# Differential attention with routed experts: one maximum for both score rows of a unit, and the guard of the denominators twice a batch

## The reference

```python
s1 = einsum('bhqd,bhkd->bhqk', q, k1) * SCALE      # causal: masked above the diagonal
s2 = einsum('bhqd,bhkd->bhqk', q, k2) * SCALE
attn = softmax(s1) - sigmoid(lambda_logit) * softmax(s2)
denom = maximum(sum(abs(attn), axis=-1), 1e-6)
out = einsum('bhqk,bhkd->bhqd', attn / denom, v) @ Wo.T
x = layernorm(x + out)
x = layernorm(x + experts(x) + x)                  # router, top 2 of 8, silu hidden layer of 512
```

## Time and profile before

| what | us |
| --- | --- |
| median of 3 runs | 1231.5 (1228.81 to 1231.53) |
| the profiled execution, its own time | 1223.18 |
| its span | 1221.3 |
| mean granted TensorE clock of the span | 0.952 of 2.4 GHz |

### The profile page before, as it was taken

The page is one execution under the profiler, slowest core; times in us unless marked ns, Lnnn a source line. Parts: engine busy times, 40 slices in busy tenths (PEclk is TensorE's granted clock), DMA queues, the critical chain, the costliest instruction groups (busy, mean ns, idle before and its releaser), DMA issues.

```text
span 1221.3 us, 29361 instructions
## 1 busy us (share of the span) xinstructions
PE 1103.2 (90%) x8786; PEld 725.7 (59%) x8786; DVE 1044.4 (86%) x2722; ACT 915.2 (75%) x2882; POOL 834.0 (68%) x1245
## 2 busy tenths in 40 slices
PE   3788869999899989999899997999899998999897
PEld 1355536666556655666556665666556665566565
DVE  1688788988999899999999899999999999898664
ACT  1688868888688877888688876888678886787232
POOL 2599976776768757877667776777677777677100
PEclk8577779999999999999999999999999999999899
DMA  7503400232005200142003300052002410000000
GB/s 213 126 14 80 99 1 3 62 82 48 1 14 118 70 2 2 36 110 57 1 14 86 89 15 1 21 125 57 1 2 57 89 48 1 19 1 2 1 10 9
DMA packets 62142, 54.66 MB, mean 45 GB/s; under 512 B 6050, under 2 KB 59938, under 8 KB 61986
## 3 DMA queue, kind: packets, MB, share of 16 engines
q1 hardware_dynamic: 61986, 52.78, 17.8%
HBM read 37.03 MB, written 15.73 MB: 43 GB/s over the span
## 4 chain that ended last, share of the span: by engine, by line
PE 66%; DVE 18%; issue 7%; POOL 4%; ACT 2%; SPq 1%; DMA 1%; DVEq 0%; POOLq 0%; ACTq 0%
PE side L809 14%; PE side L803 13%; PE trans L883 12%; PE scores L853 8%; PE heads L872 7%; DVE neg_max L723 6%; PE scores L855 4%; DVE abs_sum L734 3%; PE scores L803 2%; PE scores L809 2%; POOL exps L445 2%; PE side L773 2%; DVE hT L686 1%; DVE xh L566 1%; POOL exps L441 1%
## 5 line engine op out<-in xcount | busy, mean ns | idle before, releaser
L491 ACT ACTIVATE exps<-scores,neg_max 128x256 f32<-128x256 f32 (+3 forms) x1024 | 537.9, 529 | 97.5 <-DVE neg_max L723 80.8
L723 DVE TENSOR_REDUCE neg_max<-scores 128x1 f32<-128x256 f32 (+3 forms) x1024 | 448.7, 479 | 72.8 <-PE scores L855 69.3
L445 POOL TENSOR_TENSOR exps<-exps 128x384 f32<-128x384 f32 (+3 forms) x512 | 444.7, 868 | 42.7
L441 POOL TENSOR_SCALAR exps<-exps,inv_l,lam_l 128x384 f32<-128x384 f32 (+3 forms) x512 | 313.6, 613 | 141.2 <-DVE inv_l L714 138.4
L853 PE MATMUL scores<-stack 72*128 72x256 bf16 (+3 forms) x1024 | 274.1, 314 | 17.5 <-DMA stack<-parts_dram 13.5
L809 PE MATMUL side<-w_sb,hT 128*128 128x128 f32 x1816 | 253.6, 283 | 29.5 <-DVE acc L698 18.1
L883 PE MATMUL trans<-ident,exps 128*128 128x128 f32 x1280 | 254.9, 300 | 22.8 <-ACT diffT L499 19.4
L499 ACT ACTIVATE diffT<-trans 128x384 f32<-128x384 f32 (+3 forms) x512 | 223.4, 436 | 52.9 <-PE trans L883 52.1
L809 PEld LDWEIGHTS side<-w_sb,hT 128*128 128x128 f32 x1816 | 222.6, 192 | 63.7 <-DVE acc L698 29.9
L803 PE MATMUL side<-xnT,w_sb 128*128 128x512 f32 x458 | 247.2, 621 | 1.8 <-ACT xnT L526 1.0
L883 PEld LDWEIGHTS trans<-ident,exps 128*128 128x128 f32 x1280 | 150.4, 147 | 134.7 <-issue 102.5
(11 more groups left out here) (94 smaller groups left out, 685.2 us busy)
## 6 DMA issues: line engine op xcount, KB each, us to landing
stack<-parts_dram SPq DMA_DIRECT2D x288, 96.0 KB
parts_dram<-parts SPq DMA_DIRECT2D x104, 128.0 KB, 2.4
x_in<-x_dram SPq DMA_DIRECT2D x8, 256.0 KB, 4.5
w_sb<-w_dram SPq DMA_DIRECT2D x1, 2048.0 KB, 9.1
x_res<-x_dram SPq DMA_DIRECT2D x8, 256.0 KB, 4.5
o_dram<-y_out SPq DMA_DIRECT2D x8, 256.0 KB, 3.4
wq_sb<-wqT_dram SPq DMA_DIRECT2D x1, 64.0 KB
wq_sb<-wk1T_dram SPq DMA_DIRECT2D x1, 64.0 KB
```

Of the source, the lines that this page charges most:

```text
L441: nc.gpsimd.tensor_scalar(diff[:, q % 2, j, 0:w], exps[:, q % 2, 1, j, 0:w], inv_l2[:, q % 2, j:j + 1], lam_l1[:, q % 2, j:j + 1], ALU.mul ...
L445: nc.gpsimd.tensor_tensor(diff[:, q % 2, j, 0:w], diff[:, q % 2, j, 0:w], exps[:, q % 2, 0, j, 0:w], ALU.subtract).then_inc(diff_done.sem, 1)
L491: nc.scalar.activation(exps[:, q % 2, k, j, 0:w], scores[:, u % 2, k, 0:w], ACT.Exp, bias=neg_max[:, q % 2, j, k:k + 1], accum_out=sums[:, ...
L723: nc.vector.tensor_reduce(neg_max[:, q % 2, j, k:k + 1], scores[:, u % 2, k, 0:w], AX.X, ALU.max, negate=True).then_inc(max_done.sem, 1)
```

## The change

- **Scores.** Where both rows of a unit fit one bank (t = 0 and 1, w = 128 and 256), they are written side by side into the bank of k = 0, by one matmul of 2w columns over both sets of keys, and one of 256 columns for both masks, from a mask that is now held twice. Before it PE waits for both exponentials of unit u - 2. For t = 2 and 3 the four matmuls stay as they were, each k in its bank, and each k waits for its own exponential, save after a packed unit. In every case `score_done` now counts once a unit, after the last of its matmuls.
- **Maxima.** One reduction over both rows, of 2w numbers, with one wait for `score_done` and one `max_done`. Both exponentials of the unit wait for it.
- **Denominators.** `sums` and `abs_sum` are kept for the whole batch; guard and reciprocal run twice a batch, over 32 numbers a row, in slot 40 for the first half and in slot 8 of the next batch for the second, in place of 16 times over 4 numbers.

```diff
-        sums = sb("sums", [P, 4, 2, QUAD])
+        sums = sb("sums", [P, 2, NG, NT, QUAD])
...
+        def packed(t):
+            return 2 * (t + 1) * P <= 512
+
+        def score_pair(u):
+            t = tile_of(u // QUAD)
+            w = (t + 1) * P
+            if packed(t):
+                return scores[:, u % 2, 0, 0:2 * w].rearrange("p (k c) -> p k c", k=2)
+            return scores[:, u % 2, :, 0:w]
...
-                            act.wait_ge(max_done.sem, max_done.after(n, 2 * u + k + 1))
-                            nc.scalar.activation(exps[:, q % 2, k, j, 0:w], scores[:, u % 2, k, 0:w],
+                            act.wait_ge(max_done.sem, max_done.after(n, u + 1))
+                            nc.scalar.activation(exps[:, q % 2, k, j, 0:w], score_pair(u)[:, k, :],
...
-                        q, j = divmod(u, QUAD)
-                        if j == QUAD - 1:
-                            dve.wait_ge(abs_done.sem, abs_done.after(n, 2 * (q + 1)))
-                            nc.vector.scalar_tensor_tensor(out=guard[:, :], in0=sums[:, q % 4, 0, :], scalar=DENOM_MIN,
-                                                           in1=abs_sum[:, q % 2, :], op0=ALU.mult, op1=ALU.max)\
+                        i, last_of_part = divmod(u + 1, DEN_UNITS)
+                        if last_of_part == 0:
+                            part = slice((i - 1) * DEN_G, i * DEN_G)
+                            dve.wait_ge(abs_done.sem, abs_done.after(n, (u + 1) // 2))
+                            nc.vector.scalar_tensor_tensor(out=guard[:, :, :, :], in0=sums[:, 0, part, :, :],
+                                                           scalar=DENOM_MIN, in1=abs_sum[:, part, :, :],
...
-                        for k in range(2):
-                            dve.wait_ge(score_done.sem, score_done.after(n, 2 * u + k + 1))
-                            nc.vector.tensor_reduce(neg_max[:, q % 2, j, k:k + 1], scores[:, u % 2, k, 0:w], AX.X,
-                                                    ALU.max, negate=True).then_inc(max_done.sem, 1)
+                        dve.wait_ge(score_done.sem, score_done.after(n, u + 1))
+                        nc.vector.tensor_reduce(neg_max[:, q % 2, j, :], score_pair(u), AX.X,
+                                                ALU.max, negate=True).then_inc(max_done.sem, 1)
...
+                        if packed(t):
+                            pe.wait_ge(exp_done.sem, exp_done.after(n, 2 * (u - 2) + 2))
+                            nc.tensor.matmul(pair, queries, stack[:, 1:3, QUAD * g + j, 0:w], start=True, stop=False)
+                            nc.tensor.matmul(pair[:, :, w - P:w], ident_bf[:, :], causal_bf[:, :, :],
                                              start=False, stop=True).then_inc(score_done.sem, 1)
+                        else:
+                            before = u - 2 if u >= 2 else u - 2 + UNITS
+                            for k in range(2):
+                                freed = 2 if packed(tile_of(before // QUAD)) else k + 1
+                                pe.wait_ge(exp_done.sem, exp_done.after(n, 2 * (u - 2) + freed))
```

More of the change, by code:

```diff
@@ L58 @@
 LAG_SIDE = 1
+DEN_PARTS = 2
+DEN_G = NG // DEN_PARTS
+DEN_UNITS = UNITS // DEN_PARTS
 SIDE = {}
@@ L179, in build @@
         diffT = sb("diffT", [P, 2, QUAD, T])
-        abs_sum = sb("abs_sum", [P, 2, QUAD])
-        guard = sb("guard", [P, QUAD])
+        abs_sum = sb("abs_sum", [P, NG, NT, QUAD])
+        guard = sb("guard", [P, DEN_G, NT, QUAD])
         inv_den = sb("inv_den", [P, NT, NH])
@@ L392, in body @@
                     for g in range(NG):
[L394 removed]
+                        sp.wait_ge(score_done.sem, score_done.after(n - 1, (g + 1) * QUAD * NT))
                         for z in range(3):
@@ L733, in body @@
                         dve.wait_ge(diff_done.sem, diff_done.after(n, u + 1))
-                        nc.vector.tensor_reduce(abs_sum[:, q % 2, j - 1:j + 1], diff[:, q % 2, j - 1:j + 1, 0:w], AX.X,
+                        nc.vector.tensor_reduce(abs_sum[:, q // NT, tile_of(q), j - 1:j + 1], diff[:, q % 2, j - 1:j + 1, 0:w], AX.X,
                                                 ALU.add, apply_absolute_value=True).then_inc(abs_done.sem, 1)
                     for n, u in units(b, stages, slot, LAG_DEN):
-                        q, j = divmod(u, QUAD)
-                        if j == QUAD - 1:
-                            dve.wait_ge(den_done.sem, den_done.after(n, 2 * q + 1))
-                            nc.vector.reciprocal(inv_den[:, tile_of(q), q // NT:NH:NG], guard[:, :])\
-                                .then_inc(den_done.sem, 1)
+                        i, last_of_part = divmod(u + 1, DEN_UNITS)
+                        if last_of_part == 0:
+                            dve.wait_ge(den_done.sem, den_done.after(n, 2 * i - 1))
+                            nc.vector.reciprocal(
+                                inv_den[:, :, :].rearrange("p t (j g) -> p g t j", g=NG)[:, (i - 1) * DEN_G:i * DEN_G, :, :],
+                                guard[:, :, :, :]).then_inc(den_done.sem, 1)
                     if slot == LAG_PV and "attention" in stages:
@@ L850, in body @@
                             pe.wait_ge(stack_in[g].sem, stack_in[g].after(n, 3 * len(WINDOWS)))
-                        for k in range(2):
-                            pe.wait_ge(exp_done.sem, exp_done.after(n, 2 * (u - 2) + k + 1))
-                            nc.tensor.matmul(scores[:, u % 2, k, 0:w], stack[:, 0, QUAD * g + j, t * P:(t + 1) * P],
-                                             stack[:, 1 + k, QUAD * g + j, 0:w], start=True, stop=False)
-                            nc.tensor.matmul(scores[:, u % 2, k, w - P:w], ident_bf[:, :], causal_bf[:, :],
-                                             start=False, stop=True).then_inc(score_done.sem, 1)
+                        pair = score_pair(u)
+                        queries = stack[:, 0, QUAD * g + j, t * P:(t + 1) * P]
+                        if packed(t):
+                            pe.wait_ge(exp_done.sem, exp_done.after(n, 2 * (u - 2) + 2))
+                            nc.tensor.matmul(pair, queries, stack[:, 1:3, QUAD * g + j, 0:w], start=True, stop=False)
+                            nc.tensor.matmul(pair[:, :, w - P:w], ident_bf[:, :], causal_bf[:, :, :],
+                                             start=False, stop=True).then_inc(score_done.sem, 1)
+                        else:
[3 more added lines that the diff above has]
+                                pe.wait_ge(exp_done.sem, exp_done.after(n, 2 * (u - 2) + freed))
+                                nc.tensor.matmul(pair[:, k, :], queries, stack[:, 1 + k, QUAD * g + j, 0:w],
+                                                 start=True, stop=False)
+                                last = nc.tensor.matmul(pair[:, k, w - P:w], ident_bf[:, :], causal_bf[:, k, :],
+                                                        start=False, stop=True)
+                            last.then_inc(score_done.sem, 1)
                     for task, n, bank in side_tasks(b, stages, slot):
```

27 lines of the change are left out of this document (13 added, 14 removed).

## The result

The changed kernel takes 1247.95 us in the median of 4 runs (1244.45 to 1251.33), beside 1230.43 for the kernel before in its 4. The ratio is 1.0143, with a 95% interval of 1.0111 to 1.0175: 17.5 us slower. I had forecast 1230 and a range up to 1245. The profiled execution of the changed kernel has a span of 1242.7 us at a mean granted TensorE clock of 0.970, so a lower clock isn't the reason. The profile of before shown above is one of the shortest executions of that kernel: its own runs on the chips of the experiments go from 1222 to 1243 us.

A forecast was written before the change was run, and what follows sets the result against it. Steady batches were taken as bound by PE, but by DVE in the 54 us norms and router stretch, batch 0 by round trips. With 5.6 us less in seven batches and 4 more in batch 0: 1230 us, range 1226 to 1235, eight-in-ten 1212 to 1245.

The forecast's parts named there:

- 0.07 us a pair: DVE maxima: one reduction in place of two saves 0.07 us whatever the width, 4.5 us a batch over 64 units.
- The first event of the chain: Unit 44, t = 3, PE stretch: first exponential starts 0.8 us later, of which 0.5 us stay.
- the delay wins: Rival: lost time of 2.5 us a steady batch and 6 in batch 0 outweighs the gains; 1242 us, chance 0.32.
- 7 x (2.3 + 0.3 - 1.8): Seven steady batches: DVE gains 2.3, PE gain 0.3, less delays 1.8 us a batch; 5.6 us less in all.
- Both of the signs that I had named: Signs of being wrong: PE stretch staying at 61 us (then faster), or batch 0 alone losing over 8 us.
- I take 4 us more, between 1 and 6.: Batch 0: trip scores, maximum, exponential, scores 0.3 us longer at t = 2 and 3, 16 times; 5 us, partly absorbed.
- POOL takes up some of it: Batch 0: POOL, busy 88 of 103 us, was to absorb part of the 5 us of longer round trips.
- The 1.8 us: Steady batch, later first exponentials in four t = 3 runs: 0.6 + 0.4 + 0.8 us lost; ends 0.5 and 2.5.
- The 0.3 us a batch: PE, packed units: two fewer matmuls in each of 32 units, at 0.005 to 0.01 us each, save 0.3 us a batch.
- weight loads are paid for: Rival: the two mask loads a packed unit drops save PE 2.6 us a batch; 1212 us, chance 0.05 (named "pairs").
- the terms of the stretch of norms: Steady batch, where DVE is the bound: maxima up to 1.5 and guards with reciprocals, totalled as 3.1 us if everything counted.
- slow banks: Rival: reduction slower over two PSUM banks, 0.1 us each at t = 2 and 3, 3 us a batch; 1245 us, chance 0.04.

The follow-up runs named there:

- e2: Kernel before, with the first exponential waiting for both maxima and the first maximum for the scores of both k; no work changed: ratio 1.0221.
- e5: Changed kernel with no unit packed, so four score matmuls a unit into two banks; one maximum and rare guards left: ratio 1.0182 to the kernel before.
- e1: Kernel before, with the first exponential of a unit also waiting for the second maximum; no work changed: ratio 1.0195.
- e9: Kernel before, with the first exponential also waiting for the second maximum at t = 3 alone; no work changed: ratio 1.0119.
- e4: Kernel before, with guard and reciprocal twice a batch and nothing else changed: ratio 0.9948.
- e3: Kernel before, with one maximum over both rows in place of two; scores still in two banks by four matmuls, guards each quad: ratio 1.0172.
- e12: Changed kernel with ACT's copy of diffT moved ahead of both exponentials in its slot: ratio 1.0115 to the kernel before.

## Why the prediction was wrong

**What held.** The work: 0.07 us a pair, no price for two banks, a guard in its new place that is still blocked behind POOL about every other time, but 16 times and not 128, DVE 8 us a batch less busy where I had said 10. The place, in steady batches: the t = 3 units lose. The first event of the chain, the exponential 0.1 us behind a reduction that starts late, is in the trace as worked out. And "the delay wins" was the right rival; I gave it 0.32 and 1242, and it took 1248.

**What failed, in the terms of the sum.** The sum was 7 x (2.3 + 0.3 - 1.8) less and 4 more, or 1.6 us less; measured are 17.5 more. In the traces batch 0 has 10.5 us more where I had 4, and a later batch 1.6 more where I had 0.8 less, so that seven of them make the greater part of the error. By the ratios, delays and gains have about equal shares. I had 17.6 us of delays (7 x 1.8 + 5), and e2, which has the waits and saves no work, took 27 more. I had 19.2 us of gains (7 x 2.6 + 1), and the changed kernel is only 10 us faster than e2. Both shares are uncertain by some 6 us. Both of the signs that I had named came: batch 0 lost over 8 us, and the stretch ruled by PE kept its length. From the second I had concluded that the kernel would be faster. It was not: there packing gives back what t = 3 loses (62.9 us, and 63.4 in e5 without packing), and the loss stands in the norms stretch, 1.9 us longer where I had said 1 to 2 shorter.

**The first step: batch 0.** "I take 4 us more, between 1 and 6." The trace has 10.5 more, and e2, with waits alone, 12.3. I priced the trip over two units at 0.3 us longer, sixteen times at t = 2 and 3. A trip, two units, got longer by 0.56 us at t = 3, by 0.37 at t = 2, and by 0.49 at t = 1, for which I had nothing; t = 0 gave 1 us back. What is put in a row there is DVE's start, later by the second scores (0.5 us at the clock of that stretch), and the first exponential, later by the second maximum (0.6 us). Nor had I seen the trip over the copy and the transpose, which in batch 0 ends 16.0 us of PE's idle time, beside 3.6 us for the one over the exponentials. "POOL takes up some of it" has nothing in the traces for it: POOL is busy for 90 of 113 us.

**The second: the delays of a steady batch.** The 1.8 us were four single events, each worked out with all other engines kept where they were. e1's 3.2 us a later batch (142.5 less 139.3) is the measure, or 2.8 in e9 with t = 3 alone; with the trace of before being a short one, about 2.5 and 2. The missing part is what the second engine hands back: a late exponential makes a late `tanh`, a late `hT`, and so a late maximum two slots on, and it makes a late copy, a late transpose and late scores. My ends were 0.5 and 2.5, and the measure is near the upper one.

**The third: gains that I added up.** Guards alone bring 0.5% (e4), and the merged maximum against its waits another 0.5% (e2 to e3). But e5, which has both, isn't faster than e3, which has one: 1.0182 and 1.0172. With e3 and e4 as terms the sum would be 1.012, and packing would make it less, where the changed kernel has 1.0143. The likely reading is that once the waits set the pace, time taken from DVE buys little, also in the stretch of norms where DVE had been the bound: a loss takes away the condition of a gain on the same path. It isn't shown, as the intervals of e3 and e5 leave room for the 0.5%.

**The fourth: PE.** The 0.3 us a batch was too small; quads at t = 0 and 1 are shorter in the changed kernel than in e5 by 0.32 and 0.19 us, 2 us a batch, of which its longer quads at t = 3 (9.17 and 9.01) take back a part. I had taken the spacing of short matmuls and not looked at what stands behind them. The rival "weight loads are paid for" had about the size (2.6) for a reason that may be next to the right one. That softened the result, and didn't turn it.

Two sums of the prediction don't come out as written: the terms of the stretch of norms add up to 3.0, not 3.1, and "3 us a batch" for slow banks gives more than 1245 unless only part of it counts. Neither changes the forecast.

**What stays open.** At t = 3 in steady batches ACT's own work, about 2 us a unit with `tanh`, is close to the time of a slot, and so are both trips, over the copy and the transpose and over the exponentials. e12 shows only that opening the first makes the second the longer one. A second buffer for transposes or a third one for scores would separate them; neither was tried.

## What to carry to other kernels

Where a pair of steps runs on two engines in turn (maximum and exponential, twice a unit), the split is a pipeline: merging it saves the fixed cost of one instruction, 0.07 us here, and gives up the overlap of one half, 0.6 us at 512 keys. Merge where the half is short or the next engine idles, and keep the split where it is long and that engine is near full: here that alone turned 1.4% slower into 0.7% faster. In a sum, ask of every gain whether it still lies on the path once the losses are in, and follow a delay round every loop that it enters, until it meets itself: here the one over the copy and the transpose as well.

## What was not expected of the hardware

A float32 matmul of 512 columns behind the scores took 0.86 us on PE's chain where it took 0.91, when the matmul before it had 256 columns and not 128, both at the full granted clock. And eight times the numbers cost a guard next to nothing beside what POOL costs it: 0.18 us was the shortest over 32 numbers and 0.145 the shortest over 4, while seven of the 16 over 32 numbers took 0.32 to 0.91 us and ended with an instruction of POOL.
